# Seven block products in two more groups of the shared experts, and the weight sums that they need moved to items 11 to 27

## The reference

```python
for e in range(2):                                   # shared experts
    h = silu(x_flat @ s_w1[e].T) * (x_flat @ s_w3[e].T)
    shared_out += h @ s_w2[e].T
s = sigmoid(router_in @ W_router.T)                  # 8 experts, the best 2 of each token
_, topk_idx = top_k(s + router_bias, 2)
for e in range(8):                                   # routed experts
    h = gelu(x_flat @ r_w1[e].T); routed_out += h @ r_w2[e].T * gates_full[:, e:e+1]
out = (shared_out / 2 + routed_out) / 4
```

## Time and profile before

| | |
|---|---|
| time, median of 3 runs | 1931.31 us (1929.91 to 1931.38) |
| time of the profiled execution | 1928.58 us |
| its span, first to last instruction | 1926.9 us |
| granted TensorE clock, mean | 0.994 |
| PE busy | 1888.6 us (98%) |
| DVE busy | 1161.5 us (60%) |
| ACT busy | 913.3 us (47%) |

### The profile page before, as it was taken

The page is one execution under the profiler, slowest core; times in us unless marked ns, Lnnn a source line. Parts: engine busy times, 40 slices in busy tenths (PEclk is TensorE's granted clock), DMA queues, the critical chain, the costliest instruction groups (busy, mean ns, idle before and its releaser), DMA issues. The chain is left out here.

```text
span 1926.9 us, 46866 instructions
## 1 busy us (share of the span) xinstructions
PE 1888.6 (98%) x18676; PEld 1220.2 (63%) x18676; DVE 1161.5 (60%) x2542; ACT 913.3 (47%) x1939; POOL 156.6 (8%) x160
## 2 busy tenths in 40 slices
PE   8999989999999999999999999999999999999997
PEld 7999954444444434444444444457777777799996
DVE  6666646554788655412111115678788887688887
ACT  4444445434122344434333335434455544588886
POOL 0000000000000000211111102111111120000000
PEclk8999999999999999999999999999999999999999
DMA  7033347776353565899999967665554467133232
GB/s 309 14 131 131 133 143 200 236 198 201 129 174 134 182 219 164 175 253 209 216 222 204 202 139 238 186 188 156 147 158 136 138 176 247 58 132 81 47 57 47
DMA packets 306607, 313.47 MB, mean 163 GB/s; under 512 B 228904, under 2 KB 247470, under 8 KB 299503
## 3 DMA queue, kind: packets, MB, share of 16 engines
q1 hardware_dynamic: 293310, 267.01, 48.3%
q0 software_dynamic: 13104, 43.79, 10.1%
HBM read 191.46 MB, written 73.66 MB: 138 GB/s over the span
## 5 line engine op out<-in xcount | busy, mean ns | idle before, releaser
L1276 PE MATMUL sh_p<-xh,arena 128*128 128x512 f16 x1280 | 382.6, 381 | 7.8 <-ACT sh_gated L1552 4.8
L1347 PE MATMUL p<-sh_h_hi,arena 128*128 128x512 f16 x1024 | 304.8, 379 | 1.0 <-DVE sh_h_lo L1932 1.0
L1276 PE MATMUL sh_p<-xl,arena 128*128 128x512 f16 x640 | 243.6, 381 | 0.0
L2293 DVE SCALAR_TENSOR_TENSOR ro_hs<-ro_h,fac,ro_hs 128x512 f16<-128x512 f32 x71 | 53.4, 752 | 296.4 <-ACT ro_hs L2279 296.4
L1276 PEld LDWEIGHTS sh_p<-xh,arena 128*128 128x128 f16 x1280 | 125.1, 98 | 160.7 <-ACT sh_gated L1552 5.3
L2236 PE MATMUL ro_py<-arena,ro_ht 128*128 x852 | 195.0, 379 | 1.1 <-DMA ro_ht<-ro_hs 1.1
L1347 PE MATMUL p<-sh_h_lo,arena 128*128 128x512 f16 x512 | 194.1, 379 | 0.0
L1523 ACT CAST sh_h_hi<-sh_gated 128x512 f16<-128x512 f32 x128 | 79.1, 618 | 234.7 <-DVE sh_gated L2025 208.2
L1347 PEld LDWEIGHTS p<-sh_h_hi,arena 128*128 128x128 f16 x1024 | 96.5, 98 | 107.1 <-DVE sh_h_lo L1932 1.7
L2236 PEld LDWEIGHTS ro_py<-arena,ro_ht 128*128 128x128 f16 x852 | 83.4, 98 | 101.8 <-issue 1.6
L2025 DVE SCALAR_TENSOR_TENSOR sh_gated<-sh_p,fac,sh_gated 128x512 f32<-128x512 f32 x80 | 60.0, 750 | 99.1 <-PE sh_p L1276 98.9
(11 more groups left out here) (334 smaller groups left out, 3962.2 us busy)
## 6 DMA issues: line engine op xcount, KB each, us to landing
stage<-in_shared_w SPq DMA_DIRECT2D x29, 768.0 KB, 5.5
routed_rows<-xres SPq DMA_DIRECT2D x71, 256.0 KB, 2.7
stage<-in_norms_r SPq DMA_DIRECT2D x16, 1024.0 KB, 5.0
stage<-in_routed_w SPq DMA_DIRECT2D x16, 1024.0 KB, 6.4
stage<-in_norms SPq DMA_DIRECT2D x14, 1024.0 KB, 5.4
arena<-x SPq DMA_DIRECT2D x12, 1024.0 KB, 6.0
x<-xres SPq DMA_DIRECT2D x16, 512.0 KB, 2.6
x_rows<-arena SPq DMA_DIRECT2D x8, 1024.0 KB, 8.9
```

Source lines behind the costliest of these rows:

```text
L1276: mm = nc.tensor.matmul(p1[u % P1][:], arena[:, w:w + P], x[slot(gl)][:, :, k, :], start=(j == 0), stop=(j == 3 * KD - 1))
L1347: mm = nc.tensor.matmul(p2[m][:], arena[:, w:w + P], h[n % 2][:], start=(i == 0 and j == 0), stop=(i == HID - 1 and j == 2))
L2293: nc.vector.scalar_tensor_tensor(hs[t % TURNS][:, D:2 * D], h[t % 2], fac[:, 3:4], hs[t % TURNS][:, 0:D], ALU.mult, ALU.subtract).then_inc ...
```

## The change

In the first half the last two groups (items 32 to 63, `SEVEN = 2 * HID`) are computed by the seven block products too. For that:

- The 16 weight sums are made in items 11 to 26 (`MIX_AT`), one in each item, so that ACT and DVE work on them in items 12 to 27 and SP stores them in items 13 to 28. `mix` becomes two buffers; `mixed` stays one buffer. The quarter s3 of each tile goes back into the arena in SP's items 17 to 32 (`load_s3`), and s1, s2 and s4 are loaded again for each item from 32 on (`load_mixed`, 384 KB). The quarter that s3 overwrites in tile 0 is kept in memory (`a21`) and put back in the routed part.
- Two of the four groups are split into x blocks (`raw_block`, `split_block`, `low_block`) in place of `split_x`.
- `row_sums` goes from DVE to ACT: four activations with Abs and an accumulated output instead of one reduction.
- `list_part` becomes three wide DVE instructions instead of 16.
- The route is one item later; the 16 matrices go to items 48 to 60, 62, 63, one in each, and the last one (`LATE_MATRIX`) is split at the start of the routed part. The routed weights' two matrices of an expert change places.
- The fourth tile of gathered rows is fetched at the start of the routed part, as its place holds sums until then.

The core of the diff (the changes of index from HID to SEVEN and the renamed buffers are left out):

```diff
-MIX_AT = tuple(range(14, 24, 2)) + tuple(range(40, 62, 2))
+MIX_AT = tuple(range(11, 11 + HID))
+MATRIX_AT = {15: 0, 11: 1, 12: 2, 13: 5, 14: 9}
+LATE_MATRIX = 10
...
+    SEVEN = 2 * HID if first_part else HID
...
-            mix, mixed = sb("mix", [P, MIXES * QUARTER]), sb("mixed", [P, MIXES, 2, QUARTER], F16)
+            mix = [sb("mix", [P, MIXES * QUARTER])[:], keep["spare"][:].bitcast(F32)]
+            mixed = sb("mixed", [P, MIXES, 2, QUARTER], F16)
...
-        ROUTE_AT = look_at(LOOKS)
+        ROUTE_AT = look_at(LOOKS) + 1
...
-        plain = lambda n: first_part or n < HID
+        plain = lambda n: n < SEVEN
...
                 def load_mix(t):
-                    if t:
-                        sp.wait_ge(mix_lo, t)
-                    sp.dma_start(mix[:], src["shared_w"][t][:, 0:2 * PIECE]).then_inc(mix_in, 16)
+                    if t >= 2:
+                        sp.wait_ge(mix_lo, t - 1)
+                    sp.dma_start(mix[t % 2], src["shared_w"][hidden(t)][:, 0:2 * PIECE]).then_inc(mix_in[t % 2], 16)
...
                 def load_s3(i):
-                    sp.wait_ge(p1_filled, 2 * i + 2)
+                    sp.wait_ge(p1_filled, 2 * (SEVEN - HID + i) + 2)
+                    if first_part:
+                        sp.wait_ge(mix_stored, 16 * (i + 1))
...
+                    if first_part and n == SEVEN - 1:
+                        load_mixed(SEVEN)
+                        load_mixed(SEVEN + 1)
+                    if SEVEN < n < ITEMS - 1:
                         load_mixed(n + 1)
...
+                def row_sums(b):
+                    q = LOADED + b
+                    act.wait_ge(stage_in[q % 2], in_stage(q))
+                    for r in range(KD):
+                        part = stage[q % 2][:, r * D:(r + 1) * D]
+                        total = nc.scalar.activation(part, part, ACT.Abs, accum_out=keep["sums"][:, NORMS_S + b, r:r + 1])
+                    total.then_inc(stage_done, 1)
...
-                    for i in range(LISTED):
-                        nc.vector.tensor_scalar(at_lane[u % 2][:, i, :], lanes, part_f[:, c, t:t + 1], token[:, t:t + 1], ALU.is_equal, ALU.mult)
-                        one = nc.vector.tensor_scalar(in_tile[u % 2][:, i, 0:SLOT_TILES], starts, whole_f[:, c, t:t + 1], None, ALU.is_equal)
+                    nc.vector.tensor_tensor(spots, starts.unsqueeze(1).broadcast_to([P, LISTED, SLOT_TILES]), each(whole_f[:, c, t:t + LISTED], SLOT_TILES), ALU.is_equal)
+                    nc.vector.tensor_tensor(at_lane[u % 2], lanes.unsqueeze(1).broadcast_to([P, LISTED, P]), each(part_f[:, c, t:t + LISTED], P), ALU.is_equal)
+                    nc.vector.tensor_tensor(spots, spots, each(token[:, t:t + LISTED], SLOT_TILES), ALU.mult).then_inc(list_ready, 1)
...
-                    for t in range(ROWS_RING):
+                    for t in range(ROWS_RING - 1):
                         nc.gpsimd.indirect_dma_start(row_ring(keep, t), None, dram["xt"], bass.IndirectOffsetOnAxis(ap=token_of[:, t:t + 1], axis=0)
...
+                act.wait_ge(*late_loaded)
+                for a in range(late_at, late_at + MATRIX, MATRIX // 2):
+                    nc.scalar.activation(arena[:, a:a + MATRIX // 2], late_raw[:, a - late_at:a - late_at + MATRIX // 2], ACT.Copy, scale=scl[:, 5:6]).then_inc(late_hi, 1)
```

More of the change, by code:

```diff
@@ L996, in shared_part @@
         look_at = lambda a: 2 + 3 * a
-        ROUTE_AT = look_at(LOOKS)
+        ROUTE_AT = look_at(LOOKS) + 1
         NORM_AT = ROUTE_AT + 1
         SCALE_AT = NORM_AT + NORMS_R
-        order = [b for b in range(2 * EXPERTS) if matrix_end(b) is None] + [b for b in range(2 * EXPERTS) if matrix_end(b) is not None]
-        E_AT = SCALE_AT + 3
+        matrix_at = {b: (PART_GROUPS - 1) * HID + (MATRIX_AT[b] if matrix_end(b) is None else matrix_end(b) + 1) for b in range(2 * EXPERTS)}
+        order = sorted(matrix_at, key=lambda b: matrix_at[b])
+        assert order[-1] == LATE_MATRIX and SCALE_AT + 3 < matrix_at[order[0]]
         def split_at(j):
-            last = matrix_end(order[j])
-            return E_AT + j if last is None else (PART_GROUPS - 1) * HID + (last - 1) + 1
+            return matrix_at[order[j]]
         def stage_load(q):
@@ L1437, in _ @@
                         last_three(n)
-                    elif n and (first_part or n < HID - 1):
+                    elif n and n < SEVEN - 1:
                         second(n - 1)
-                if not first_part:
-                    second(ITEMS - 2)
+                second(ITEMS - 2)
                 second(ITEMS - 1)
@@ L1564, in _ @@
                         split_tile(n + AHEAD)
-                    if not first_part and i in BLOCK_AT and gl + 1 < PART_GROUPS:
+                    if i in BLOCK_AT and in_sevens(gl + 1):
                         split_block(gl + 1, BLOCK_AT.index(i))
@@ L1575, in _ @@
                             scores()
-                        for j in range(2 * EXPERTS):
+                        if NORM_AT <= n < NORM_AT + NORMS_R:
+                            row_sums(n - NORM_AT)
+                        for j in range(2 * EXPERTS - 1):
                             if n == split_at(j):
@@ L1615, in _ @@
                         gate_left(n)
-                if not first_part:
-                    gate_right(ITEMS - 1)
-                    high_h(ITEMS - 1)
+                gate_right(ITEMS - 1)
+                high_h(ITEMS - 1)
                 if first_part:
-                    for j in range(2 * EXPERTS):
+                    for j in range(2 * EXPERTS - 1):
                         if split_at(j) >= ITEMS:
@@ L2048, in _ @@
                         mix_sums(MIX_AT.index(n - 1))
-                    if not first_part and gl + 1 < PART_GROUPS:
+                    if in_sevens(gl + 1):
                         for r in range(len(RAW_AT)):
```

224 lines of the change are left out of this document (144 added, 80 removed).

## The result

| | before | after |
|---|---|---|
| median of the runs | 1930.61 us (4 runs) | 1968.18 us (4 runs) |
| profiled execution | 1928.58 us | 1969.49 us |
| its span, granted clock | 1926.9 us, 0.994 | 1967.8 us, 0.980 |

The ratio is 1.0199 [1.0187, 1.0211]. The direction was forecast, the size was not: 1968 lies above the upper end of the range (1965), and the change costs 38 us by the medians and 41 by the profiled executions, where 16.8 were worked out.

The account below looks back on a forecast made before the run. PE was taken to set the pace. The terms -26.5 + 34.3 + 3.2 + 2.5 + 1.3 + 2 = +16.8 us gave 1945.4 us for the profiled execution and 1948 us in runs; the range was 1931 to 1965.

Parts of the forecast that it names:

- Savings: 32 items fall from 7.77 to 7.175 us (19.0) and item 52's loss goes (7.5): -26.5 us together.
- The sums in items 12 to 27: First half: `mix_high` waits for the one buffer's store, looks take 30.6 us for PE's 24.11: +34.3 us (17.5 to 47.1).
- The distances: Steps between `mix_high`s in looks: 10.1 us behind first items, 14.3 behind second, 6.2 behind third, 13.3 in item 17.
- Rival 1: Items 12 to 27: stores land within an item and no `mix_high` is late; 1914 us in runs, chance 0.09.
- rival 2: Second items of looks: the 1 MB load holds the store less, steps of 10.1 us; 1931 us, chance 0.11.
- rival 4: Slower still: third items at 9.4 us (1961), matrices and quarters colliding at every item (1955), or table loads (1958); chance 0.21.
- Block products' first and last items and the split in item 63: First half from item 32: 3.2 us of waits (1.0 to 6), plus 1.3 for the split ahead of DVE's last gates (0 to 2.6).
- Matrices and quarters: Items from 48 on: quarters queue behind each matrix's load on SP and land late; +2.5 us (0 to 10).
- Start of the routed part: The fourth tile's late gather takes 4.4 us and SP holds its transpose, with three tiles as PE's cover: +2 us (0 to 4).
- Row sums on ACT and wide lists: Items 28 to 43: four activations stand ahead of `gate_left`, DVE gets shorter lists; nothing either way.
- The +10 us of table loads: Abs between Silus might make ACT load function tables, 2.57 us in each of 16 items; taken as none.

Follow-up runs that it names:

- the square: Changed kernel with one or two buffers of mixed: 1968.2 and 1942.6 us with transposes, 1944.1 and 1932.1 with none from look 4 on.
- the last version: Changed kernel with two buffers, spread sums, reordered gathers and transposes (1926.3 us), then each matrix's load put behind the next item's quarters: 1924.2 us.
- each edit: Changed kernel with gathers held until row 3 is transposed: 1969.4 us; then also the first three hidden-row transposes ahead of later rows': 1966.4 us.

## Why the prediction was right in direction and short in size

*Savings, right.* -26.5 forecast, -26.4 measured; 7.17 us an item.

*The sums in items 12 to 27: right in mechanism, +41.1 for +34.3.* It is the largest term, and its size was too small. The chain of waits, the place of the pauses and their releasers came as described, and the two-buffer run shows the store's landing to be worth 25.6 us by itself. The distances, single rows of the kernel before, did not hold: the steps were up to 2.1 us longer, 8.0 over the twelve. Of this 3.8 us are a later issue of the store. SP now issues transfers of the change ahead of it that the step left out: the copy of the kept quarter in item 14, and the load of a quarter s3 from item 17 on (`load_s3`, line 1163; the store is line 1143):

```profile
450.57 0.41 SPq L1163 DMA_DIRECT2D arena<-mixed  x1
451.02 0.47 SPq L1143 DMA_DIRECT2D mixed<-sh_mixed  x1
```

Later landings make 2.7, over half of it in one store of 8.2 us in item 21; third items make 1.0, and the rest is the step from landing to start. Behind the last look 1.4 us were lost at the lower clock, where 2.7 were put. Also, the 1 MB load was taken as the price of second items: the run with the store ahead of it shows that the delay only changes its owner. The four transposes were in the distances; the square shows that their hold on SP is what makes one buffer cost 25.6 us and not 12.0. Rival 1 (stores don't hold) is refuted by the waits and rival 2 (the load holds less) by the second items' steps of 14.4 to 16.4 us; rival 4's 9.4 us in third items did not come.

*Block products' first and last items and the split in item 63, +7.5 for +4.5.* The chain at the end took 2.6 us of waiting, where the second half has 1.0; the first quarters took 2.8. The router's chain on DVE (line 1467, 1.7 us) was late as the sums ran into its items: that wait was not forecast.

*Matrices and quarters, +10.5 for +2.5 (0 to 10).* This is the largest excess, 8.0 us. The step failed by an omission: it priced the quarters behind a matrix's load, but not behind the two transposes in item 58, which hold SP for 5.09 us. That item alone is 6.3 us. What was priced, a matrix ahead of quarters, is item 49 (2.1) and about 2 us in items 52 to 59; the last version took most of it away.

*Start of the routed part, +7.6 for +2 (0 to 4).* The price was one gather's landing (4.4 us) less PE's cover. In the trace the transpose behind it landed 8.4 us after its issue, with three more gathers in flight. That these hold it is shown (3.0 us without them). That this saves time is not: each edit moved the wait on. By the trace the 7.6 us are the wait of 5.0, 1.7 and 2.1 at the lower clock (granted 0.50 from 816.6 to 820.0 us, behind the 2.6 us of waiting in the last items, and from 836.3 to 840.5 us, behind the 5.0), less 1.1 that the kernel before waits here (7.7 in all).

*Row sums on ACT and wide lists, nothing, right.* Items 35 to 43 are each 0.59 to 0.60 us shorter than before. In ACT's groups (busy, mean ns, idle before), 272 to 830 us, Abs comes 64 times with its read of the sum, and Silu's line has the two table loads that it had before:

```profile
L1526 ACT ACTIVATE stage<-stage 128x512 f32<-128x512 f32 x64 | 39.3, 615 | 0.0
L1526 ACT ACTIVATION_READ_ACCUMULATOR stage<-stage 128x1 f32 x64 | 12.0, 187 | 0.0
L1609 ACT ACT_TABLE_LOAD x2 | 2.6, 1283 | 0.0
```

The +10 us of table loads did not come. The Trainium skill ("ScalarE: Activation LUTs", section "Table sets: the hidden batching unit") says that abs is in every table set; the trace agrees.

*The range.* Four terms erred, all upward: the sums and the quarters by leaving transfers out of SP's queue, the routed part by a price from a quieter stretch, the first items by leaving out the router's chain. Two stayed within their own bounds (the sums below 47.1, the block products with the split in item 63 below 8.6); the quarters (10.5 over 10) and the routed part (7.6 over 4) did not. The range left out the sum of two parts of rival 4; the outcome was three smaller excesses together (3.0, 8.0 and 5.6 us) on top of 6.8 us in the main term.

## What to carry to other kernels

When a step that loads and stores is put into every item, write down first what the one issuing queue does ahead of each store and load, transposes and the change's own small transfers included, and price each landing by what is issued ahead of it, not by the row of a quiet stretch. A single buffer whose reuse waits for a store makes a chain of landings, and moving one transfer ahead of another in the same queue hands the delay on; a second buffer, or every other item, breaks the chain. Ask of every transfer that a queue issues late what is queued behind it: two transposes ahead of a quarter cost 6.3 us, as much as ten shorter items saved.

## What the hardware showed unexpectedly

- A transpose in DMA holds the queue that issues it. Four of 128x512 f16 hold SP for 5.1 us, where four copies of four bytes a partition hold it for 2.5; in the one-buffer kernel this is nearly all that they cost (21.1 of 21.9 us).
- They also take more of the engines' listed time than their bytes say. Leaving out 36 of them in 130 us lowered the share by 0.17, 22 us of all sixteen engines, while other transfers moved more, not less; that is at least 0.6 us for each 128 KB, an estimate, where the 400 GB/s of that stretch's fullest slices would give 0.33 (the size is that of the 128x512 f16 tile). The share is no measure of room, though: it reads 1.14 from 830 to 845 us in the changed kernel, and 0.92 in the last version, whose PE hardly waits.
- In the rows shown the same 512 KB store landed in 3.1 to 12.3 us, by what had been issued ahead of it.
- The pauses of PE ahead of the looks' logits (2.3 to 8.1 us) were each followed by a stretch at the lower clock: after the one of 6.33 us the granted clock is 0.50 from 479 to 485 us. The pauses of 1.7 and 1.8 us for the router and for quarters (547.7 and 597.6 us) were not. Over the looks the mean is 0.91, and with the pauses mostly gone (two buffers, no transposes) 0.99.
